# LSTM and GRU in one kernel: narrow products for the bound of x, the last output in natural form, unread products in the last waits

## What is computed

```python
# layer 0 (LSTM), h = cond, c = 0
a = x[:, t] @ Wx + b + h @ Wh            # 2048 columns: i, f, o, g
c = sigmoid(f) * c + sigmoid(i) * tanh(g)
h = sigmoid(o) * tanh(c)
y[:, t] = x[:, t] + h
# layer 1 (GRU), g = 0, its input is y, vz, vr, vh are products of cond
z = sigmoid(y[:, t] @ W_z + g @ U_z + vz)
r = sigmoid(y[:, t] @ W_r + g @ U_r + vr)
n = tanh(y[:, t] @ W + (r * g) @ U + vh)
g = (1 - z) * g + z * n
out[:, t] = y[:, t] + g
```

## Time and profile before

| | us |
|---|---|
| median of 3 runs | 1243.46 (1242.91 to 1243.78) |
| the profiled execution | 1244.18 |
| its span, first to last instruction | 1242.4 |
| PE busy | 1205.5 (97%) |
| DVE busy | 872.4 (70%) |
| ACT busy | 445.0 (36%) |
| POOL busy | 278.0 (22%) |
| mean granted clock of TensorE | 0.989 |

### The profile page before, as it was taken

How to read it: one execution, slowest core, us unless ns; L and a number is a source line. 1 busy time by engine, 2 the same in 40 slices (tenths; PEclk the granted TensorE clock), 3 DMA queues, 4 the chain that set the end, 5 groups by cost and what they waited for, 6 DMA issues and landing times.

```text
span 1242.4 us, 67987 instructions
## 1 busy us (share of the span) xinstructions
PE 1205.5 (97%) x31013; PEld 763.8 (61%) x31013; DVE 872.4 (70%) x2681; ACT 445.0 (36%) x1078; POOL 278.0 (22%) x520
## 2 busy tenths in 40 slices
PE   5889999999999999999999999999999999999996
PEld 1457666666666666666666666666666666666664
DVE  2568877777777777777776777777777777677765
ACT  5555233333333333333333333333333333333332
POOL 3100222222212222222222221222222222222221
PEclk9899999999999999999999999999999999999998
DMA  9900100111110111110011111011111001110001
GB/s 304 317 9 12 20 10 14 21 20 20 21 19 6 20 21 21 20 21 12 12 21 21 20 21 20 5 19 20 21 21 21 13 11 21 20 20 12 12 8 24
DMA packets 142000, 39.50 MB, mean 32 GB/s; under 512 B 135760, under 2 KB 136016, under 8 KB 140688
## 3 DMA queue, kind: packets, MB, share of 16 engines
q1 hardware_dynamic: 140016, 34.49, 12.9%
q0 software_dynamic: 640, 0.53, 0.2%
q10 hardware_dynamic: 1056, 0.13, 0.1%
HBM read 26.74 MB, written 8.39 MB: 28 GB/s over the span
## 4 chain that ended last, share of the span: by engine, by line
PE 93%; SPq 3%; DVE 2%; DMA 1%; issue 1%; ACT 0%; POOLq 0%; POOL 0%; DVEq 0%
PE ps_l L780 51%; PE ps_g L780 38%; PE ps_g L789 3%; SPq L239 2%; DMA o_area<-in_L_cond_C_dram 1%; PE ps_l L789 1%; SPq L243 1%; PE ps_bound L822 0%; DVE wh L538 0%; DVE u L538 0%; DVE zr L541 0%; SPq L248 0%; SPq L250 0%; PE ps_c L789 0%; ACT zr L457 0%
## 5 line engine op out<-in xcount | busy, mean ns | idle before, releaser
L780 PE MATMUL ps_l<-wh,h2T 128*32 128x512 f16 x5952 | 344.4, 380 | 3.3 <-DVE wh L538 3.3
L780 PE MATMUL ps_l<-wx,x2T 128*32 128x512 f16 x5952 | 342.8, 379 | 0.0
L780 PE MATMUL ps_g<-w,y2T 128*32 128x384 f16 x5760 | 256.2, 327 | 0.0
L780 PEld LDWEIGHTS ps_l<-wx,x2T 128*32 128x32 f16 x5952 | 160.6, 97 | 134.2
L780 PEld LDWEIGHTS ps_l<-wh,h2T 128*32 128x32 f16 x5952 | 154.6, 97 | 138.7 <-DVE wh L538 3.6
L780 PEld LDWEIGHTS ps_g<-w,y2T 128*32 128x32 f16 x5760 | 155.3, 97 | 92.3
L320 POOL TENSOR_TENSOR yT<-xT,hT 128x128 f32<-128x128 f32 x128 | 61.9, 484 | 589.8 <-DVE hT L670 589.8
L780 PE MATMUL ps_g<-u,g2T 128*32 128x256 f16 x5760 | 178.5, 273 | 0.8 <-ACT g2T L485 0.8
L780 PEld LDWEIGHTS ps_g<-u,g2T 128*32 128x32 f16 x5760 | 154.7, 97 | 16.9 <-issue 1.2
L541 DVE SCALAR_TENSOR_TENSOR zr<-ps_g,sc,term 128x256 f32<-128x256 f32 x128 | 61.9, 484 | 108.0 <-PE ps_g L780 100.5
L304 POOL TENSOR_TENSOR o_area<-yT,gT 128x128 f32<-128x128 f32 x128 | 58.6, 458 | 307.3 <-DVE gT L763 307.3
(11 more groups left out here) (101 smaller groups left out, 1107.3 us busy)
## 6 DMA issues: line engine op xcount, KB each, us to landing
out_dram<-o_area SPq DMA_DIRECT2D x128, 64.0 KB, 2.1
x_nat<-in_x_dram SPq DMA_DIRECT2D x126, 64.0 KB, 2.7
wh<-in_L_cond_Wx_dram SPq DMA_DIRECT2D x4, 1024.0 KB, 12.0
w<-in_L_cond_Wh_dram SPq DMA_DIRECT2D x3, 1024.0 KB, 20.4
u<-in_L_cond_Wh_dram SPq DMA_DIRECT2D x1, 1024.0 KB, 26.5
stage<-in_L_cond_W_z_dram SPq DMA_DIRECT2D x1, 1024.0 KB, 8.5
stage<-in_L_cond_W_r_dram SPq DMA_DIRECT2D x1, 1024.0 KB, 8.1
stage<-in_L_cond_W_dram SPq DMA_DIRECT2D x1, 1024.0 KB, 10.3
```

Of the source, the lines that this page charges most:

```text
L780: mm = nc.tensor.matmul(bank[B * j:B * j + B, c0:c1].rearrange("p (n c) -> p n c", c=B), still(a, k), moving(b, k, j), start=opens and (a, ...
```

## The change

1. `ones16` has 32 columns, and `bound` issues four products, one for each 32-column place, with the same column of `raw`; the last of them signals.
2. The last output isn't made from yT and gT. POOL makes `y_nat`, x plus h in natural form, in tick T - 1, and behind the ticks DVE adds `g_nat` to it and writes the last quarter of `o_nat`. The last gT isn't made. The turn of group 30 and that of the first three steps of group 31 move to the head of tick T on DVE, ahead of zr's sum, each with a wait for the buffer's earlier store. SP stores group 31 in two parts: three steps (four DMAs of 48 KB) and one step (four of 16 KB).
3. `go_on(count)` issues the first steps of a product of x2T and wx into a PSUM bank that nobody reads any more: 7 steps in each of the ticks T - 1 and T ahead of the wait for rg2T, and 3 steps in tick T ahead of the wait for g2T.

```diff
-    def natural(a, t):
-        return a[:, t:t + Q, :].rearrange("b t (k j p) -> j b (t k) p", k=K, j=J)
+    def natural(a, t, count=Q):
+        return a[:, t:t + count, :].rearrange("b t (k j p) -> j b (t k) p", k=K, j=J)
...
-        ones16 = sbuf("ones16", [P, P], bf16)
+        ones16 = sbuf("ones16", [P, B], bf16)
...
# SP
             ticks(tick)
-            store(T - Q, (NG - 1) % 2, NG - 1)
+            r = (NG - 1) % 2
+            for t, count, done in ((T - Q, Q - 1, NG), (T - 1, 1, NG + 1)):
+                sp.wait_ge(o_done, done)
+                c = P * (t % Q)
+                for j in range(J):
+                    sp.dma_start(natural(out, t, count)[j], o_nat[rows(j), r, c:c + P * count].rearrange("b (n p) -> b n p", p=B)
+                                 ).then_inc(out_done[r], 16)
...
# POOL, at the end of tick
+                if t == T - 1:
+                    pool.wait_ge(h_done, T)
+                    nc.gpsimd.tensor_tensor(y_nat[:], x_nat[:, r, P * q:P * q + P], h_nat[:], ALU.add).then_inc(y_nat_done, 1)
             ticks(tick)
-            add_out(T - 1, (T - 1) % U, NG - 1)
...
# DVE
-            def turn_out(r, group):
-                dve.wait_ge(oT_done, Q * group + Q)
-                nc.vector.transpose(o_nat[:, r, :], oT[:, r].rearrange("p t c -> p (t c)")).then_inc(o_done, 1)
+            def turn_out(r, group, count=Q):
+                dve.wait_ge(oT_done, Q * group + count)
+                nc.vector.transpose(o_nat[:, r, 0:P * count], oT[:, r, 0:count].rearrange("p t c -> p (t c)")).then_inc(o_done, 1)
...
+                if t == T:
+                    for a in (NG - 2, NG - 1):
+                        dve.wait_ge(out_done[a % 2], 16 * J * (a // 2 + 1))
+                        turn_out(a % 2, a, Q if a < NG - 1 else Q - 1)
                 if gru:
...
-                if t >= 2 * Q + 1 and t % Q == (1 if t < T else 0):
+                if t >= 2 * Q + 1 and t % Q == 1 and t < T:
...
-                    if t >= LAG + 2:
-                        dve.wait_ge(oT_done, s - 1)
-                    nc.vector.transpose(gT[:, s % 2, :], g_nat[:]).then_inc(gT_done, 1)
+                    if s < T - 1:
+                        if t >= LAG + 2:
+                            dve.wait_ge(oT_done, s - 1)
+                        nc.vector.transpose(gT[:, s % 2, :], g_nat[:]).then_inc(gT_done, 1)
...
             ticks(tick)
-            dve.wait_ge(out_done[(NG - 1) % 2], 16 * J * (NG // 2))
-            turn_out((NG - 1) % 2, NG - 1)
+            dve.wait_ge(y_nat_done, 1)
+            nc.vector.tensor_tensor(o_nat[:, (NG - 1) % 2, P * (Q - 1):P * Q], y_nat[:], g_nat[:], ALU.add).then_inc(o_done, 1)
...
# PE
-                nc.tensor.matmul(ps_bound[:, r:r + 1], ones16[:], raw[:, r:r + 1], start=True, stop=True).then_inc(bound_ps, 1)
+                for j in range(J):
+                    mm = nc.tensor.matmul(ps_bound[rows(j), r:r + 1], ones16[:], raw[:, r:r + 1], start=True, stop=True)
+                mm.then_inc(bound_ps, 1)
...
+            def go_on(count):
+                product(ps_l[0], 0, GL * P, wx_of, x_of((NG - 1) % 2, Q - 1), 0, count, True, False)
...
                     done.then_inc(cond_ps, 1)
+                if t == T:
+                    go_on(3)
...
                     bound(1 - r, group + 1)
+                if t >= T - 1:
+                    go_on(7)
```

More of the change, by code:

```diff
@@ L121, in lstm_then_gru @@
         o_area = sbuf("o_area", [P, 2, 2, Q * P])
+        y_nat = sbuf("y_nat", [P, P])
         oT, o_nat = o_area[:, 0].rearrange("p r (q c) -> p r q c", q=Q), o_area[:, 1]
@@ L195, in lstm_then_gru @@
         o_done = sem("o_done")
+        y_nat_done = sem("y_nat_done")
         block = ctx.enter_context(nc.Block())
@@ L275, in _ @@
             ticks(tick)
-            store(T - Q, (NG - 1) % 2, NG - 1)
+            r = (NG - 1) % 2
[5 more added lines that the diff above has]
+                                 ).then_inc(out_done[r], 16)
             for r in range(2):
-                sp.wait_ge(out_done[r], 16 * J * (NG // 2 + 1))
+                sp.wait_ge(out_done[r], 16 * J * (NG // 2 + 1 + r))
         @block.gpsimd
```

## The result

The changed kernel takes 1233.53 us (median of 6 runs) against 1243.18 us before; the ratio of all runs is 0.9919, with an interval of 0.9906 to 0.9931 (the medians alone give 0.9922). Two more measurements gave 0.9921 (0.9908 to 0.9933) and 0.9909 (0.9896 to 0.9923), the last with one execution at 1229.91. So the change is worth about 10 us where 7.9 were forecast: faster, as said, and at the lower edge of the range. The profiled execution took 1231.82 us with a span of 1229.9, at the fast end of its runs (1231.82 to 1234.02), as that of before stood 0.7 above its median; the two spans differ by 12.5, and that is more than the kernels do.

What follows compares the result with a forecast made beforehand. PE's queue was taken to bound the kernel, with 93% of the chain of waits. Savings of 4.4 us for the bounds and 3.5 for the end, 7.9 together, gave 1235.6 us from a median of 1243.46; range 1233.2 to 1238.8.

Steps and rivals of the forecast that it cites:

- zr's sum: DVE's operation taking finished z and r products from PSUM in tick T; forecast 1231.12 in place of 1232.15, gain 1.03 us.
- The bound before: One 128-column product each fourth tick, costing PE 0.207 us because changing between widths 32 and 128 lets nothing overlap.
- The bound after: Four 32-column products cost 0.056 us, saving 0.151 each; 4.2 us for 28 steady bounds, 4.4 in all.
- 56 ns for a set of four: Cost taken for four narrow bound products, from the rg2T product: 12 sets of four in 0.67 us.
- Rival A: Narrow weight loads of the bound aren't hidden, 97 ns for a set; 6.8 us saved, 1236.7 us; chance 0.17.
- rival D: The bound's four products don't overlap, 0.54 us for a set; slower, 1250 us; chance 0.04.
- rival B: Wait and signal cost, not width; the bound stays at 0.207 us, only the end gains, 1240.0 us; chance 0.08.
- two early bounds: Bounds of ticks 4 and 8, ahead of the steady part, where PE has waits: 0.2 us together, between 0 and 0.3.
- A shorter memset of ones16 too: 0: At the start, where weights are loaded, setting fewer columns of ones16 was forecast to gain 0.
- cand: DVE's operation taking the candidate's finished product from PSUM in tick T; 0.91 behind the product for 1.29, gain 0.38 us.
- Output chain: Work behind the last cell: one 128x128 sum in place of gT's turn, ending at 1237.10 for 1238.45, gain 1.35 us.
- Rivals C and E: C: filling doesn't hold the clock, 1238.3 us, chance 0.07. E: DVE's turns late, small stores no faster, chance 0.04.

## Why the prediction came out as it did

**What bounds it: right. The bound before: right in kind, a little short.** What came off PE's queue came off the time. That the cost is the width and not the type was read from the earlier trace rows and holds. The 0.207 was taken against the mean of all ticks without a bound, in which the tick behind each bound has its last 0.01; against 4 × 9.110 the bound cost 0.222.

**The bound after: right in kind, the size off.** The step that failed is the choice of 56 ns for a set of four. It measured 25 ns, because the rg2T row that it was taken from the earlier trace rows is paced by its 128 columns of data and says nothing on one column; the row is a bound from above and was used as the value. So a bound less brings 0.198 and not 0.151: 5.35 for 27 periods, and 5.5 for 28 bounds where 4.2 were in the sum. Of these 1.3 us, 0.9 are the 56 ns and 0.4 the 0.207. Rival A's 97 ns and rival D fell, rival B too. Of the two early bounds, tick 4 gave 0.22 (41.93 to 41.71 between the bounds of ticks 4 and 8) and tick 8 nothing (38.44 to 38.43 between the bounds of ticks 8 and 12), as PE waits there: 0.2 as forecast.

**What was missing: the place of the biases.** This is the largest miss, a term put at nothing. "A shorter memset of ones16 too: 0" was true of the memset and blind to the 192 bytes by which all buffers behind it moved. Measured alone, on the kernel before, that place is worth 1.9 us (0.7 to 3.0). No rival had it, and the trace of before could not have shown it by itself.

**The end: right term by term in the traces.** zr's sum 4.94 behind the product of tick T - 1 in place of 5.98: 1.04 (forecast 1.03). cand 0.90 in place of 1.29: 0.39 (0.38). Output chain from cand's start to DVE's last 1.67 in place of 3.03: 1.36 (1.35). From there to the end of the span 3.31 in place of 3.95: 0.64 (0.7), though not as it was made up: the last store starts 1.30 behind the first in place of 1.44, so 0.14 earlier and not 0.36, and the other 0.5 lie between its start and the end. Where I was too sure is the clock: 1.41 of it was read from one execution of the kernel before, and the six ends without filling have a mean of 79.3 and not 79.7, so that over many runs the end is worth some 3.0, not 3.5. Rivals C and E fell: the clock stayed at 1.00, and DVE's turns ended 0.44 early.

**The sum.** 5.5 + 0.2 for the bounds, 3.0 for the end, 1.9 for the place make 10.6; measured were 10.1, 9.8 and 11.3 by the ratios, 9.7, 9.8 and 10.5 by the medians. The forecast's 7.9 lacked 1.3 of the bound and the 1.9, and had 0.5 too much for the end. Its range reached down to the measured time for another reason, a bound that costs nothing, and not for the place of the buffers, so that the time lies in it is in part luck. Of the 3.65 by which the two traces differ ahead of the first steady bound, 0.2 are the bounds and 1.8 the place (170.3 against 172.1). The other 1.6 is put down to the spread from execution to execution and not shown by itself; three traces of the changed kernel have their first bound at 39.9, 40.1 and 41.2 and the first steady one at 169.1 to 170.0, and the ten traces with the biases 64 bytes beyond have the latter at 171.0 to 173.1.

## What to carry to other kernels

Where TensorE is full of products of 32 columns, issue the odd small product at that width too: here going to another width and back cost 0.20 us, the products 6 ns each. When an edit changes the size of a buffer, check what else moves with it, and test it by a pad in the old kernel that changes no instruction; and give buffers that DMA fills in 128-byte pieces a place on a multiple of 128 bytes, above all those loaded beside what the start waits for (in every kernel here where the biases lay so they were on a multiple of 256 too, so that is the safe choice). What an idle gap costs by the clock should be read from several executions: in one it was 1.7 us more than in another with the same end. Filling such a gap pays only where the clock would fall, and should delay nothing: one step did as well as three and cost nothing.

## What the runs showed of the hardware that was not expected

Sixteen products of 32 columns with one column of data cost 0.10 us in a full queue, 6 ns each. A second product of 128 columns right behind the first costs 0.026, and two of 64 columns between products of 32 cost 0.24, hardly less than two of 128 with 0.25. DMAs in pieces of 128 bytes take longer when the SBUF side lies 64 bytes beyond a multiple of 128: SP's queue took 12.9 to 13.0% of the engines' time with x_nat and o_area so placed and 12.2 to 12.4% with o_area or both on a multiple, for the same 34.5 MB, and with the biases so placed the 20 us in which they come in beside the weights had 298 to 311 GB/s against 335 to 348. The Trainium skill, DMA: Bandwidth & Descriptors, "How a descriptor splits into AXI transactions", has a rule of this kind for reads: a descriptor that doesn't start on a multiple of 256 bytes has bytes fetched that nobody uses, which cost beats. Only the stores read from SBUF here, the loads of biases write to it, and of writes that section says nothing; no run here tells 128 from 256. After a wait of 2.03 us the granted clock was down to 0.50 in one execution and stayed at 1.00 in another; with waits of 0.53 and less it was at 1.00 up to PE's last product in all thirteen traces with the filling.
